# The last 42 value columns and the last 42 gate columns of a gated FFN share one tile of the up projection

## The reference

```
DIM_INNER = int(DIM * 4 * 2 / 3)                 # 682
for i in range(DEPTH):                           # 6
    x = attn_layer(shift_tokens(x), Wqkv[i], q_scale[i], k_scale[i], Wo[i]) + x
    x = ffn_layer(shift_tokens(x), ln_g[i], ln_b[i], W1[i], b1[i], W2[i], b2[i]) + x

def ffn_layer(...):
    xn = (x - mu) / jnp.sqrt(var + 1e-05) * g + bln
    hg = xn @ W1 + b1                            # 256 -> 2*682: values, then gates
    a, gate = jnp.split(hg, 2, -1)
    return a * jax.nn.gelu(gate, approximate=False) @ W2 + b2
```

## Time and profile before

| | |
|---|---|
| median of 3 runs | 3540.26 us (3533.38 to 3541.16) |
| profiled execution, its own time | 3541.11 us |
| span from the first to the last instruction | 3539.3 us |
| mean granted TensorE clock | 0.980 |
| busy share PE / PEld / DVE / ACT / POOL | 88 / 74 / 71 / 65 / 41 % |

### The profile page before, as it was taken

How to read it: one execution, slowest core, us unless ns; L and a number is a source line. 1 busy time by engine, 2 the same in 40 slices (tenths; PEclk the granted TensorE clock), 3 DMA queues, 4 the chain that set the end, 5 groups by cost and what they waited for, 6 DMA issues and landing times.

```text
span 3539.3 us, 80127 instructions
## 1 busy us (share of the span) xinstructions
PE 3121.6 (88%) x24104; PEld 2603.2 (74%) x24104; DVE 2523.9 (71%) x8851; ACT 2316.6 (65%) x6640; POOL 1465.6 (41%) x1053
## 2 busy tenths in 40 slices
PE   6688998888899888999988899888989988898996
PEld 5567777777777777777776777776777767777775
DVE  3466777777777777777777777677767777777773
ACT  3357666666666666666666766766676667666663
POOL 3344444434444344444343434433444434344440
PEclk9899999999999999999999999999999999999998
DMA  4200000111000111000011000012000011100000
GB/s 129 86 9 11 10 19 12 32 51 38 12 10 19 33 39 40 19 12 10 20 46 56 11 19 12 10 32 68 22 10 10 19 33 39 33 15 16 17 17 17
DMA packets 94293, 98.78 MB, mean 28 GB/s; under 512 B 8516, under 2 KB 81056, under 8 KB 94112
## 3 DMA queue, kind: packets, MB, share of 16 engines
q1 hardware_dynamic: 94112, 96.61, 8.9%
HBM read 73.54 MB, written 16.78 MB: 26 GB/s over the span
## 4 chain that ended last, share of the span: by engine, by line
PE 48%; DVE 20%; ACT 15%; issue 11%; DVEq 1%; ACTq 1%; POOL 0%; DMA 0%; SPq 0%; POOLq 0%
PE project L780 10%; PE wide L833 8%; PE acc L848 5%; DVE with_sin L1121 5%; ACT probs L1001 4%; PE acc L810 4%; PE score L863 4%; DVE sums_sq L1118 4%; PE mix L887 3%; DVE masked L1199 3%; PE score L865 3%; PE turned L872 3%; PE mix L889 2%; DVE sums_sq L1123 2%; ACT L964 2%
## 5 line engine op out<-in xcount | busy, mean ns | idle before, releaser
L780 PE MATMUL project<-w_qkv,xT 128*128 128x512 f32 x3456 | 944.3, 412 | 58.3 <-DVE xT L1101 38.0
L1034 POOL TENSOR_TENSOR query_scale<-sums_sq,half 128x8 f32<-128x8 f32 x192 | 412.9, 2151 | 1370.8 <-DVE sums_sq L1123 1365.8
L1001 ACT ACTIVATE probs<-masked,shift 128x128 f32<-128x128 f32 (+1 forms) x1536 | 648.2, 426 | 434.0 <-DVE shift L1199 431.6
L780 PEld LDWEIGHTS project<-w_qkv,xT 128*128 128x128 f32 x3456 | 623.9, 193 | 191.5 <-DVE xT L1101 46.0
L1199 DVE CUSTOM_DVE_ANT_0 masked<-score,mask,query_scale 128x128 f32<-128x128 f32 (+1 forms) x1536 | 519.3, 375 | 309.2 <-PE score L865 291.9
L833 PE MATMUL wide<-nT,w_up 128*128 128x256 f32 x3456 | 489.5, 292 | 164.9 <-ACT gates L964 81.6
L833 PEld LDWEIGHTS wide<-nT,w_up 128*128 128x128 f32 x3456 | 442.0, 194 | 214.4 <-ACT gates L964 103.0
L986 ACT COPY probsT<-turned 128x320 f32<-128x320 f32 x768 | 328.7, 428 | 326.0 <-PE turned L875 325.9
L1037 POOL TENSOR_TENSOR inv_norm<-sums_sq,half 128x8 f32<-128x8 f32 x192 | 411.8, 2145 | 228.2 <-DVE sums_sq L1123 228.2
L1207 DVE TENSOR_SCALAR probs<-probs,inv_sums 128x128 f32<-128x128 f32 (+1 forms) x1536 | 410.1, 309 | 0.0
L1212 DVE TENSOR_TENSOR oT<-mix,oT 128x256 fp32r<-128x256 f32 x384 | 162.0, 422 | 210.0 <-ACT oT L994 198.0
(11 more groups left out here) (128 smaller groups left out, 5966.8 us busy)
## 6 DMA issues: line engine op xcount, KB each, us to landing
staging<-in_w_qkv SPq DMA_DIRECT2D x24, 768.0 KB
y_in<-y_scratch SPq DMA_DIRECT2D x48, 256.0 KB, 2.8
res<-y_scratch SPq DMA_DIRECT2D x48, 256.0 KB, 2.9
y_scratch<-res SPq DMA_DIRECT2D x40, 256.0 KB, 2.2
staging<-in_w_up SPq DMA_DIRECT2D x12, 682.0 KB
staging<-in_w_out SPq DMA_DIRECT2D x6, 1024.0 KB
xn<-res SPq DMA_DIRECT2D x48, 112.0 KB, 2.3
staging<-in_w_down SPq DMA_DIRECT2D x6, 640.0 KB
```

The lines of the kernel that those rows point to most:

```text
L780: last = pe.matmul(project[(x - 1) % 2][:], xT[a][:, h, t * P:(t + 1) * P], w_qkv[w][:, h, c, g, :], start=(h == 0 and (a, w) == PASSES[0] ...
L1001: last = act.activation(probs[:, t % 4, at:at + b - a], masked[:, t % 2, a:b], ACT.Exp, bias=shift[:, t % 2, i:i + 1], scale=-1.0, accum_o ...
L1034: pool.tensor_tensor(query_scale[:, u // 2, g * GROUP_HEADS:(g + 1) * GROUP_HEADS], sums_sq[:, u, :], half[:, 0:GROUP_HEADS], ALU.pow).the ...
```

## The change

The full tiles stay: 5 of gates, 5 of values. The 42 + 42 columns that are left go into one shared tile: the values' rest on partitions 0 to 41, the gates' rest on partitions 64 to 105. It is made as k = 1 of the third gate fill. So a step has 11 tiles and 66 matmuls, and fill 7 (value 2) has one tile with 6 matmuls. ACT applies Gelu to the gates' part of the shared tile (partitions 64 to 105) and now signals `gated`. A new DVE item `("rest",)`, first in tick 10's list, waits for it, reads the values' part of the shared tile from PSUM (partitions 0 to 41), adds the bias and multiplies by the gates on partitions 64 to 105. It writes partitions 0 to 41 of `gates[:, 5, :]`, and it is what frees the bank for value 0. Value 2 has one scalar_tensor_tensor in place of two. The W1 pieces 2 of values and gates are split in two parts each (256 and 84 elements per partition in place of 340). The gate bias of the last tile is rolled by 64 partitions on the host.

```diff
+FULL = FFN - FFN_REST
+GATE_REST = 64
+W1_COLS = 2 * FULL + P
...
-    10: [("rotate", 0, 2), ("turn", 0, 0)],
+    10: [("rest",), ("rotate", 0, 2), ("turn", 0, 0)],
...
-            for a in range(0, FFN, 2 * P):
-                b = min(a + 2 * P, FFN)
-                at = FFN if blk == 3 else 0
+            at, rest = (FULL, 2 * FULL + GATE_REST) if blk == 3 else (0, 2 * FULL)
+            for a in range(0, FULL, 2 * P):
+                b = min(a + 2 * P, FULL)
                 pieces.append([(s[:, :, a:b], self.up[0][:, :, at + a:at + b], self.up[1][:, :, at + a:at + b])])
+            pieces[-1].append((s[:, :, FULL:FFN], self.up[0][:, :, rest:rest + FFN_REST], self.up[1][:, :, rest:rest + FFN_REST]))
...
-                    for k in range(2):
-                        col = (2 * i + k) * P + (FFN if kind == "gate" else 0)
+                    for k in range(1 if x == 7 else 2):
+                        col = (2 * i + k) * P + (FULL if kind == "gate" else 0)
...
                         j = 2 * i + k
-                        last = act.activation(gates[:, j, :], wide[:, k, :], ACT.Gelu,
-                                              bias=params[:, FFN_TILES + j:FFN_TILES + j + 1])
-                    last.then_inc(wide_read, 1)
+                        rows = slice(0, P) if j < FFN_TILES - 1 else slice(GATE_REST, GATE_REST + FFN_REST)
+                        last = act.activation(gates[rows, j, :], wide[rows, k, :], ACT.Gelu,
+                                              bias=params[rows, FFN_TILES + j:FFN_TILES + j + 1])
+                    last.then_inc(wide_read if i < 2 else gated, 1)
...
+                elif kind == "rest":
+                    dve.wait_ge(params_loaded, s.layer * 32 + 32)
+                    dve.wait_ge(gated, f + 1)
+                    j = FFN_TILES - 1
+                    dve.scalar_tensor_tensor(gates[0:FFN_REST, j, :], wide[0:FFN_REST, 1, :], params[0:FFN_REST, j:j + 1],
+                                             gates[GATE_REST:GATE_REST + FFN_REST, j, :], ALU.add, ALU.mult).then_inc(wide_read, 1)
                 elif kind == "value":
                     i = item[1]
                     dve.wait_ge(wide_filled, f * WIDE_FILLS + 5 + i)
-                    if i == 0:
-                        dve.wait_ge(params_loaded, s.layer * 32 + 32)
-                        dve.wait_ge(wide_read, f * WIDE_FILLS + 4 + 1)
-                    for k in range(2):
+                    for k in range(2 if i < 2 else 1):
```

More of the change, by code:

```diff
@@ L31 @@
 GROUP = GROUP_HEADS * HEAD_DIM
-W1_COLS = 2 * FFN + FFN_TILES * P - FFN
+FULL = FFN - FFN_REST
+GATE_REST = 64
+W1_COLS = 2 * FULL + P
 BAND0, BAND1 = P, P + WINDOW
@@ L487, in _ @@
             for part in W.up:
-                pool.memset(part[:, :, 2 * FFN:W1_COLS].bitcast(FP32), 0.0)
+                pool.memset(part[:, :, 2 * FULL:W1_COLS].bitcast(FP32), 0.0)
             for i, s in LN_ORDER:
@@ L631, in layers @@
         ln_floor = sem("ln_floor")
-        wide_filled, wide_read = sem("wide_filled"), sem("wide_read")
+        wide_filled, wide_read, gated = sem("wide_filled"), sem("wide_read"), sem("gated")
         xn_high, xn_low = sem("xn_high"), sem("xn_low")
@@ L1156, in dense @@
                     dve.wait_ge(wide_filled, f * WIDE_FILLS + 5 + i)
-                    if i == 0:
-                        dve.wait_ge(params_loaded, s.layer * 32 + 32)
-                        dve.wait_ge(wide_read, f * WIDE_FILLS + 4 + 1)
-                    for k in range(2):
+                    for k in range(2 if i < 2 else 1):
                         j = 2 * i + k
-                        rows = P if j < FFN_TILES - 1 else FFN_REST
-                        last = dve.scalar_tensor_tensor(gates[0:rows, j, :], wide[0:rows, k, :], params[0:rows, j:j + 1],
-                                                        gates[0:rows, j, :], ALU.add, ALU.mult)
+                        last = dve.scalar_tensor_tensor(gates[:, j, :], wide[:, k, :], params[:, j:j + 1], gates[:, j, :],
+                                                        ALU.add, ALU.mult)
                     last.then_inc(wide_read, 1)
@@ L1275 @@
     b1 = a["L0_ffn_b1"]
+    gate_bias = columns(b1[:, FFN:])
+    gate_bias[:, :, -1] = np.roll(gate_bias[:, :, -1], GATE_REST, axis=1)
     arrays = {
@@ L1291 @@
         "b_down": a["L0_ffn_b2"],
-        "params": np.concatenate([columns(b1[:, :FFN]), columns(b1[:, FFN:]), columns(a["L0_ffn_ln_g"]),
+        "params": np.concatenate([columns(b1[:, :FFN]), gate_bias, columns(a["L0_ffn_ln_g"]),
                                   columns(a["L0_ffn_ln_b"])], axis=2),
```

## The result

| | before | after |
|---|---|---|
| median of 6 runs each, us | 3536.34 (3531.83 to 3541.16) | 3552.40 (3547.55 to 3557.89) |
| ratio, 95% interval | | 1.0045 (1.003 to 1.0059) |
| profiled execution, us (span) | 3541.11 (3539.3) | 3547.55 (3545.7) |
| a plain step, median of 30, us | 66.95 | 67.15 |

The kernel has become slower by 10.6 to 20.9 us; 11.4 us was forecast. One matmul in twelve of the up projection is gone, and it costs time. The profiled execution of after is the quickest of its six, so it shows only 6.4 us of that.

The account below looks back on a forecast made before the run. DVE's chain through L1171 was taken to set down 1, with 0.37 us of slack against PE. Plain steps 7.6, exchange steps 1.9, split pieces 1.0 and last steps 0.9 made 11.4 us: 3552 us, range 3540 to 3562.

Parts of the forecast that it names:

- DVE's slack against PE: Ahead of down 1 in a plain step: DVE's chain through L1171 could end only 0.37 us before PE is free.
- Rival 2: Tick 13: DVE's chain does not set down 1, so plain steps gain 0.37 us each; 3526 us; chance 0.12.
- D = 0.58 us: Room `rest` takes in DVE's queue in tick 10, delaying all behind it; bounds 0.395 with overlap, 0.55 to 0.62 without.
- Rival 1: `rest` in tick 10 still overlaps its DVE neighbours, taking 0.395 us; whole change 3 us, 3544; chance 0.20.
- Rival 4: `rest` itself takes more, 0.8 us of DVE's queue, for its two partition ranges; 21 us, 3562; chance 0.08.
- rival 3: DVE's L1171 and POOL's L1043 come apart, making the chain 0.26 us earlier; 7.4 us, 3548; chance 0.10.
- Value 0 is 0.78 us late: On PE, value 0 waits for `rest`; the stall ahead of unit (0,4) takes 0.68 us, leaving 0.10 on PE.
- Down 1 and the plain step: Down 1 starts 0.21 us later, so each of 36 plain steps is 0.21 us longer: 7.6 us.
- Exchange steps: Ten steps with a weight exchange, where DVE sets down 1 and down 2: 0.185 us longer each, 1.9 us.
- Split pieces: In five steps exchanging W1, two pieces become two ops each, about 0.1 us more per piece on DVE and ACT: 1.0 us.
- last steps: The last two steps, where DVE and PE take turns and `rest` lies open: about 0.9 us for both.
- The sum: Whole kernel: 7.6 + 1.9 + 1.0 + 0.9 = 11.4 us slower, from the profiled 3541.1 to 3552 us.

Follow-up runs that it names:

- e4: Changed kernel without `rest`; the last Gelu is written to partitions 0 to 41, so value 0 waits for ACT; 3516.77 us, 0.9938 of before.
- e1: Changed kernel with `rest` multiplying by partitions 0 to 41 of the fifth gate tile, so all its operands start at partition 0; 3537.30 us, 0.9996 of before.
- e2: Changed kernel with `rest` moved from the head of tick 10 to the end of tick 9, where DVE is idle; 3515.01 us, 0.9946 of before.
- e6: Changed kernel with `rest` done twice in tick 10, the first time into a spare tile; 3576.94 us, 1.012 of before.
- e3: Changed kernel with value 2 again making a second tile of 6 matmuls that nothing reads; 3555.86 us, 1.0051 of before.
- e8: Changed kernel with 42 unused columns behind W1's rows, giving them the 1450 columns of before; one run, 3557.60 us against 3542.09.

## Why the prediction was right, step by step

**DVE's slack against PE is 0.37 us, and no more.** Right. Without `rest` (e4) down 1 moves up by 0.42 us, though PE has 0.70 us less to do, and then stands still for 0.36 us; 0.36 or 0.37 of the 0.42 is the slack. Rival 2, that this chain does not set down 1, is gone: in after, e1, e2, e4 and e6 down 1 starts 0.05 to 0.06 us after L1181's end.

**D = 0.58 us.** The right end, and the term was 0.04 too low. 0.62 was the dear end that I had worked out from a gap of 0.04 on either side, and the gaps are 0.03 and 0.02 with an op of 0.48. Rival 1 (D = 0.395) fits e1 (0.40) and not the change. Rival 4 (D = 0.8) did not come: the op lasts 476 ns against 465. Nor did rival 3: L1181 lasts 0.94 us in after's plain steps and 0.69 in the exchange steps, as L1171 did.

**Value 0 is 0.78 us late, and the stall ahead of unit (0,4) takes it.** The chain of this is right: 0.75 us later in the step, 0.83 against L1222, and unit (0,4) starts 18.83 us into the step, against 18.81. What I put lower is the delay that stays on PE: value 2 starts 0.32 us later than before and not 0.10. Down 0 stands still for the low part of the first product, DVE's L1181 (0.26 us). I had seen that this can be, and that it does not set down 1; that holds, but it is why e3, with PE's full work, is 0.12 us above after: with 0.10 on PE, value 2 would have started at 26.26 and been through at 27.67, ahead of L1181. The stall is 0.52 us, where I had said about 0.6.

**Down 1 and the plain step: +0.21 us.** 0.20 measured for both (27.57 to 27.77; 66.95 to 67.15). That the two agree to 0.01 has a bit of luck in it: D is 0.04 higher, and L1222 comes 0.07 us earlier in after's step, which goes with the closer weight loads (e8, with the loads of before, has it at its old place). 36 times 0.20 is 7.2 us; forecast 7.6.

**Exchange steps: +0.185 us.** Too low. From the start of L1222 (L1212 in before) to down 2 the first exchange step of a layer takes 16.97 or 16.98 us in place of 16.70 to 16.73, the second 17.02 in place of 16.62, in all five layers. That is 0.26 and 0.40 us, 3.3 us for the ten against 1.9. The direction and the chain are right. In the step of the earlier trace rows, L1181 and L982 in after:

```profile
709.76 0.69 DVE L1181 TENSOR_TENSOR hT<-gates,hT 128x512 fp32r<-128x512 f32 x1 [0.76 <-ACT hT L980]
712.47 0.48 DVE L1173 SCALAR_TENSOR_TENSOR gates<-wide,params,gates 128x256 f32<-128x256 f32 x1
...
713.05 0.40 ACT L982 CAST hT<-gates 128x256 fp32r<-128x256 f32 x1
```

Down 2's cast is 3.29 us behind the product, in place of 712.41 - 708.74 = 3.67: the op that is gone gives back 0.38 us, as forecast (0.395), and 0.62 - 0.38 = 0.24 is nearly the 0.26. In the second, 0.16 us come on top, and they come without `rest` too: in e4 the same stretch is 16.33 and 16.39 us, 0.39 and 0.23 less than before. The third W1 piece, now two ops on ACT and two on DVE, lies in that stretch. The lengths of whole exchange steps jump by some 1.5 us from layer to layer and from kernel to kernel, so it can't be read from them how much of the 3.3 us reaches the end.

**Split pieces, 1.0 us, and last steps, 0.9 us.** The 0.1 us for each piece on either engine was a guess from no row; the 0.16 us above are what one piece was seen to cost, 0.8 us for five, and the other piece was not seen apart. The last steps can't be confirmed. The stretch ahead of the first step takes 5.3 us less in e1 than in after, and 8.5 less in e2, though the three kernels are the same there; the last two steps, too, vary by 1 to 4 us. In the last step `rest` does lie open, as forecast: PE's value 0 starts 0.05 us after its end (3529.47 + 0.47 = 3529.94; the first load at 3529.99).

**The sum.** The steps bear out 7.2 us and at most 3.3 more of the 11.4; the medians of 6 differ by 16.1 (10.6 to 20.9), the profiled pair by 6.4. 11.4 lies in the interval. Of the 16 us some 6 are not placed. That 3552 was forecast and 3552.40 measured is luck: I added 11.4 us to a profiled execution of 3541.1, and the kernel before has a median of 3536.34, so an error of 5 us in the level hides one of 5 us in the difference. The same is seen with the other sign: e2 came out 11 us below its expectation while its plain step agreed. Whether these microseconds are in the exchange steps and the front, or are only spread, stays open.

## What to carry to other kernels

Work taken off the busiest engine is worth, at most, the slack of the chain that ends next at the same place, as long as the order stays: here some 0.4 us a step of 0.70, before anything is paid for. What an operation added on another engine costs can't be told from its duration alone; its place in the queue decides (the same op cost 0.6 us a step at the head of a gapless stretch, and nothing where its engine was idle for 5.46 us), so look for the idle stretch between the time its input is ready and the time it is needed. And when a stall is left in front of an item that waits, put one that is ready ahead of it: here another 0.43 us a step, and a change that was 0.45% slower became 0.84% faster.

## What the runs showed of the hardware

A DVE op whose three inputs do not start on the same partitions (0 and 64) overlaps with neither neighbour: 0.62 us of its queue in place of 0.40, and two of them one behind the other do not overlap either (1614.55 begins 0.01 us after 1614.06 + 0.48). I had this as a bound and not as a fact. Not expected was that the reduction behind it lasts 0.69 us in after, e3, e6 and e8, and 0.67 or 0.68 in the other kernels.

The distance of PE's weight loads of W1 depends on how its tile lies in memory: for value 1 eleven intervals take 1.26 us in each of the seven kernels with rows of 1408 columns, and 1.30 in the three with rows of 1450 or 1456, at the same clock (1.00 in the steps of before and after). The row's length and the place of what lies behind W1 changed together. A start on a 64-byte boundary made no difference. The mechanism behind it is open.
